# Perceiver layer on one core: weights asked for five chunks ahead, three partition passes dealt anew, and the last stores issued by ScalarE

## What is computed

```
x = x + xattn(layernorm(x), ctx)        # top-k channel gate, conv, sigmoid
x = x + attention(layernorm(x))         # wq, wk, wv, rope, softmax, wo
h = layernorm(x)                        # x: 16 x 64 tokens x 2048, fp32
logits = h @ gate_w.T                   # 8 experts, best 2, softmax of the two
out = x + h @ base_w.T + base_b + 2 * sum_e w_e * (h @ lora_A[e].T) @ lora_B[e].T
```

## Time and profile before

| | us |
|---|---|
| median of 3 runs | 2206.58 (2205.01 to 2207.42) |
| the profiled execution's own time | 2208.99 |
| its span | 2207.2 |
| PE busy in the span | 1883.5 (85%) |
| DVE busy | 1437.4 (65%) |
| ACT busy | 1129.0 (51%) |
| POOL busy | 1113.9 (50%) |
| mean granted clock of PE | 0.957 |

### The profile page before, as it was taken

One profiled execution on the slowest core, in us unless ns is written; L12 is line 12 of the kernel. 1 busy time (PEld: TensorE's weight loads), 2 busy tenths in 40 slices (PEclk: granted clock), 3 DMA queues, 4 the chain that ended last, 5 costly groups with the idle time before them and its releaser, 6 DMA issues. The chain is left out here.

```text
span 2207.2 us, 37947 instructions
## 1 busy us (share of the span) xinstructions
PE 1883.5 (85%) x14129; PEld 1512.1 (69%) x14129; DVE 1437.4 (65%) x2226; ACT 1129.0 (51%) x2523; POOL 1113.9 (50%) x935
## 2 busy tenths in 40 slices
PE   4678789777734568999999999999999899998979
PEld 4666667666521167888878888888778787776867
DVE  5898999999999898544436401344457448655443
ACT  7999999999946674332323322223324233322212
POOL 2333344444337406666655555566645455785434
PEclk9899999999976779999999999999999999999989
DMA  9999999999801036422254442222353352675565
GB/s 388 393 384 400 356 356 352 337 346 356 318 30 77 19 98 197 130 86 87 78 183 143 143 132 96 86 86 84 128 165 126 115 205 92 209 243 164 169 213 194
DMA packets 169912, 428.56 MB, mean 194 GB/s; under 512 B 16896, under 2 KB 45824, under 8 KB 168064
## 3 DMA queue, kind: packets, MB, share of 16 engines
q1 hardware_dynamic: 164832, 416.10, 54.6%
q10 hardware_dynamic: 4608, 8.39, 1.0%
q0 software_dynamic: 288, 1.64, 0.2%
HBM read 392.51 MB, written 33.55 MB: 193 GB/s over the span
## 5 line engine op out<-in xcount | busy, mean ns | idle before, releaser
L1566 POOL TENSOR_TENSOR t<-t,t 128x512 fp32r<-128x512 f32 (+1 forms) x472 | 658.0, 1408 | 640.4 <-ACT t L1555 568.1
L2371 PE MATMUL ps<-t,t 128*128 128x512 f32 x1792 | 718.8, 401 | 36.3 <-POOL t L1566 30.9
L2372 PE MATMUL ps<-t,t 128*128 128x512 f32 x1792 | 703.9, 393 | 0.0
L2373 PE MATMUL ps<-t,t 128*128 128x512 f32 x1792 | 703.5, 393 | 0.0
L1555 ACT ACTIVATE t<-t 128x512 fp32r<-128x512 f32 (+1 forms) x472 | 281.4, 608 | 680.7 <-PE ps L2373 297.9
L883 PE MATMUL ps<-t,t 128*128 128x128 bf16 (+1 forms) x5889 | 406.4, 223 | 165.5 <-DVE t L566 154.3
L883 PEld LDWEIGHTS ps<-t,t 128*128 128x128 bf16 x5889 | 348.7, 101 | 243.8 <-DVE t L566 214.2
L566 DVE TENSOR_SCALAR t<-t,t 128x1601 bf16<-128x1601 f32 x453 | 465.6, 1054 | 6.0 <-PE ps L883 1.4
L2371 PEld LDWEIGHTS ps<-t,t 128*128 128x128 f32 x1792 | 339.8, 190 | 125.8 <-POOL t L1566 47.5
L795 ACT ACTIVATE t<-t,t 128x1601 int8<-128x1601 f32 x256 | 419.0, 1637 | 8.0 <-DVE t L725 7.9
L2373 PEld LDWEIGHTS ps<-t,t 128*128 128x128 f32 x1792 | 339.8, 190 | 73.1
(11 more groups left out here) (276 smaller groups left out, 1971.2 us busy)
## 6 DMA issues: line engine op xcount, KB each, us to landing
t<-ctxT SPq DMA_DIRECT2D x256, 800.5 KB, 6.7
t<-wqkv SPq DMA_DIRECT2D x192, 256.0 KB, 3.2
t<-wb SPq DMA_DIRECT2D x144, 256.0 KB, 3.6
t<-wo SPq DMA_DIRECT2D x128, 256.0 KB, 4.6
t<-xT SPq DMA_DIRECT2D x48, 256.0 KB, 7.0
t<-x1d SPq DMA_DIRECT2D x32, 256.0 KB, 4.9
x2d<-t SPq DMA_DIRECT2D x32, 256.0 KB, 2.0
t<-x2d SPq DMA_DIRECT2D x8, 1024.0 KB, 7.4
```

What stands on the lines that cost most here:

```text
L1566: e.tensor_tensor(wlo[r][:, 0:nk, :], raw[RAW_OF[n, 0]][:, 0:nk, :], wh[r][:, 0:nk, :].bitcast(F32), ALU.subtract).then_inc(w_lo, 1)
L2371: e.matmul(bank[:, :], wh[r][:, q, :], xl, start=(begins and q == 0), stop=False)
L2372: e.matmul(bank[:, :], wlo[r][:, q, :], xh, start=False, stop=False)
L2373: m = e.matmul(bank[:, :], wh[r][:, q, :], xh, start=False, stop=(ends and q == nk - 1))
```

## The change

1. **Five ahead.** From the first FFN chunk on SP asks at chunk n for chunk n + 5 (at the first for n + 3 to n + 5) in place of n + 3. The store of o[15] is moved ahead of that first asking. The buffers stay six, their waits too.
2. **Stores.** The 24 stores of q5 and q4 (three of the result's four quarters) go from SP to ACT (lines 2189, 2190 and 2192 of the changed kernel), after ACT's high part of the chunk three ahead. The p2 stores stay on SP.
3. **LN1_PLAN** runs the sums, centring and scaling up to four chunks earlier; the first half's gate steps stand one chunk later.
4. **LN2.** Sums of squares of columns 256 to 511 go from DVE (q2, q3) to POOL: 15 adds of 128x256, each behind the one before (ssq1 to ssq15, places 6 to 13). The steps from t1 to n3b stand one place earlier.
5. **Passes.** a2's low part goes from POOL (8 of 128x512, places 64 to 71) to DVE (2 of 128x2048, places 66 and 69); n3's low parts start at place 32, not 29; q3's eight stand three places apart (54 to 75); s1l1 at 84, not 82.
6. **Gate of the second half.** l2 and l3 at 72 and 73 (73 and 74 before), ka at 77 (78), w at 86 (83), w1 at 87 (84), r at 89 (85), r1 at 90 (86).

```diff
-LN1_PLAN = "x0 - x1 - x2 - x3 - s0 - s1 - s2 - s3 - t0 c0 - c1 c2 - c3 c4 q0 - q1 - q2 - q3 - t1 v - r g0 g1 g2 g3 - g4"
+LN1_PLAN = "x0 - x1 - x2 - x3 s0 - s1 - s2 s3 - t0 c0 c1 - c2 c3 c4 q0 - q1 - q2 - q3 t1 v - r g0 g1 g2 g3 - g4 - - - - -"
...
+for _t in range(1, 16):
+    PARTS_AT.setdefault(6 + _t // 2, []).append(f"ssq{_t}")
...
+AHEAD = 5
...
         if s == "t1":
-            e.wait_ge(l_sum, 8 * i + (8 if i < 2 else 4))
+            e.wait_ge(l_sum, 8 * i + (8 if i < 2 else 2))
+            if i == 2:
+                e.wait_ge(p_part, P_NO["ssq15"] + 1)
...
+        if s[:3] == "a2l":
+            e.wait_ge(a_part, A_NO[f"a2h{g}"] + 1)
+            e.wait_ge(v_part, V_NO["s1a1"] + 1)
+            e.tensor_tensor(ATL[:, far, :], AF1[:, far, :], XH_[:, near, :].bitcast(F32), ALU.subtract).then_inc(v_part, 1)
...
-        if s[:3] == "a2l":
-            e.wait_ge(a_part, A_NO[f"a2h{t // 4}"] + 1)
-            e.wait_ge(v_part, V_NO[f"s1a{t // 4}"] + 1)
-            e.tensor_tensor(ATL[:, 8 + t, :], AF1[:, 8 + t, :], XH_[:, t, :].bitcast(F32), ALU.subtract).then_inc(p_part, 1)
+        if s[:3] == "ssq":
+            sq = AF0[:, :, 256:512]
+            e.wait_ge(l_sq, 8 + t // 4 + 1)
+            if t > 1:
+                e.wait_ge(p_part, P_NO[s])
+            e.tensor_tensor(R1[:, 256:512], sq[:, 0] if t == 1 else R1[:, 256:512], sq[:, t], ALU.add).then_inc(p_part, 1)
...
+    def asked(n):
+
+        if n < N_FFN:
+            return [n + 3]
+        return range(n + 3 if n == N_FFN else n + AHEAD, n + AHEAD + 1)
...
+                if (p, c) == (P_FFN, 0):
+                    store(p - 1)
                 if CH0[p] + c:
-                    weights_sync(e, CH0[p] + c + 3)
+                    for n in asked(CH0[p] + c):
+                        weights_sync(e, n)
...
-                if c == 0 and p and PROJ[p - 1][0] in ("o", "p2", "q5", "q4"):
+                if c == 0 and p and p != P_FFN and PROJ[p - 1][0] in ("o", "p2"):
                     store(p - 1)
...
+    def result_scalar(e, p):
+        kind, _, i, _ = PROJ[p]
+        e.wait_ge(bank_out, BANK_NO[p] + 1)
+        if kind == "q5":
+            e.dma_start(out[:, 1, 8 + i, :], last_rc[i][:, :]).then_inc(d_end[0], 16)
+            e.dma_start(out[:, 0, 8 + i, :], U[i][:, :]).then_inc(d_end[0], 16)
+        if kind == "q4":
+            e.dma_start(out[:, 1, i, :], V[i][:, :]).then_inc(d_end[0], 16)
...
                 weights_scalar(e, CH0[p] + c + 3)
+                if p and c == 0 and PROJ[p - 1][0] in ("q5", "q4"):
+                    result_scalar(e, p - 1)
```

More of the change, by code:

```diff
@@ L143 @@
 LN_PLAN = " x0 - x1 - x2 - x3 - s0 - s1 - s2 - s3 - - t0 c0 - c1 - c2 - c3 c4 q0 - q1 - q2 - q3 - n0 t1 n1 v n2 r n3 - n4"
-LN1_PLAN = "x0 - x1 - x2 - x3 - s0 - s1 - s2 - s3 - t0 c0 - c1 c2 - c3 c4 q0 - q1 - q2 - q3 - t1 v - r g0 g1 g2 g3 - g4"
+LN1_PLAN = "x0 - x1 - x2 - x3 s0 - s1 - s2 s3 - t0 c0 c1 - c2 c3 c4 q0 - q1 - q2 - q3 t1 v - r g0 g1 g2 g3 - g4 - - - - -"
 EXPERTS_PLAN = "l0 l1 l2 l3 - l4 - u - ka kb kc x - w - w1 - r - r1"
 LN2_AT = {0: ["x0", "t0"], 1: ["x1"], 3: ["x2", "c0"], 4: ["x3"], 5: ["c1"], 7: ["c2"], 8: ["c3"], 9: ["c4"], 10: ["q0"], 11: ["q1"],
-          13: ["q2"], 15: ["q3"], 16: ["t1"], 17: ["v"], 18: ["r"], 19: ["g0"], 20: ["g1"], 21: ["g2"], 23: ["g3"]}
@@ L150 @@
-PARTS_AT = {24: ["n3a0"], 25: ["n3b0"], 26: ["n3a1", "n3h0"], 27: ["n3b1"], 28: ["n2a0", "n3h1"], 30: ["n2a1", "n2h0"],
-            31: ["s1a0"], 32: ["n2h1"], 34: ["s1a1"],
+          15: ["t1"], 16: ["v"], 17: ["r"], 18: ["g0"], 19: ["g1"], 20: ["g2"], 22: ["g3"]}
+PARTS_AT = {23: ["n3a0"], 24: ["n3b0"], 25: ["n3a1", "n3h0"], 26: ["n3b1"], 28: ["n2a0", "n3h1"], 29: ["n2a1", "n2h0"],
+            31: ["s1a0", "n2h1"], 34: ["s1a1"],
             45: ["q3a0"], 46: ["q3b0"], 47: ["q3h0"], 48: ["q3a1"], 49: ["q3b1"], 50: ["q3h1"], 52: ["n2l0"], 54: ["n2l1"],
-            62: ["a2h0"], 63: ["a2h1"], 78: ["s1h0"], 79: ["s1h1"], 80: ["s1l0"], 82: ["s1l1"]}
+            62: ["a2h0"], 63: ["a2h1"], 66: ["a2l0"], 69: ["a2l1"], 78: ["s1h0"], 79: ["s1h1"], 80: ["s1l0"], 84: ["s1l1"]}
@@ L154 @@
+for _t in range(1, 16):
+    PARTS_AT.setdefault(6 + _t // 2, []).append(f"ssq{_t}")
 for _t in range(8):
[L155 to L159, removed]
+    PARTS_AT.setdefault(32 + _t, []).append(f"n3l{_t}")
+    PARTS_AT.setdefault(54 + 3 * _t, []).append(f"q3l{_t}")
@@ L163 @@
+EXPERTS_AT = {47: ["l0"], 48: ["l1"], 72: ["l2"], 73: ["l3"], 75: ["l4"], 76: ["u"], 77: ["ka"], 79: ["kb"], 81: ["kc"], 82: ["x"],
+              86: ["w"], 87: ["w1"], 89: ["r"], 90: ["r1"]}
 PARTS = [s for k in sorted(PARTS_AT) for s in PARTS_AT[k]]
-BY_POOL = ("n3l", "q3l", "a2l")
+BY_POOL = ("n3l", "q3l", "ssq")
 V_NO = {s: k for k, s in enumerate(s for s in PARTS if s[2] != "h" and s[:3] not in BY_POOL)}
@@ L1943, in parts_gpsimd @@
     def parts_gpsimd(e, s):
-        t = int(s[3])
+        t = int(s[3:]) if s[2] != "h" else 0
         if s[:3] == "n3l":
@@ L1972, in part_there @@
         if kind == "lb" and h == 1 or kind == "q4" and i == 0 and c < 2:
-            e.wait_ge(p_part, P_NO[f"a2l{4 * c + 3}"] + 1)
+            e.wait_ge(v_part, V_NO[f"a2l{c}"] + 1)
     def experts_tensor(e, i, s):
@@ L1987, in experts_tensor @@
             if s == "l2" and i:
-                e.wait_ge(p_part, P_NO["a2l7"] + 1)
+                e.wait_ge(v_part, V_NO["a2l1"] + 1)
             bank = PS_ if i == 0 and c < 2 else b1
@@ L2108, in store @@
                 e.dma_start((x2d if kind == "o" else out)[:, h, i, :], (ev if kind == "o" else rc)[s][:, :]).then_inc(d_out[s], 16)
[L2109 to L2113, removed]
         def residual(p):
@@ L2164, in mm_sync @@
                     e.dma_start(part(AF0, k // 4, k % 4, 4), part(xT[:, 1, :, :], k // 4, k % 4, 4)).then_inc(d_xq[k // 4][0], 16)
-                if c == 0 and p and PROJ[p - 1][0] in ("o", "p2", "q5", "q4"):
+                if c == 0 and p and p != P_FFN and PROJ[p - 1][0] in ("o", "p2"):
                     store(p - 1)
-        store(len(PROJ) - 1)
         for s in range(2):
@@ L2201, in mm_scalar @@
                 e.activation(U[i][:, :], PA[p % 3][:, :], ACT.Copy).then_inc(p1_out, 1)
+        result_scalar(e, len(PROJ) - 1)
     def conv_gpsimd(e):
```

## The result

The changed kernel took 2173.67 us, the median of four runs (2172.76 to 2175.91), beside 2205.86 for the kernel before (2205.01 to 2207.42). The ratio is 0.9855, interval 0.9838 to 0.9872: faster by 32.2 us, where 42.3 were forecast. It lies inside the range, on the poor side of the middle.

A forecast was written before the change was run, and what follows sets the result against it. PE stood or ran slow for 61.8 us, through waits, mostly on late weights, and the lower clock. Terms 4.4 + 7.0 + 7.2 + 9.2 + 14.5 = 42.3 us took the median from 2206.58 to 2164 us, range 2153 to 2185.

The forecast's parts named there:

- x and q5: Stretch to 2153.8: without SP's store wait, loads wait for buffers alone; rounds of 9.13 us become 6.7, 14.5 us won.
- q3: Stretch to 2085.2: w's later place removes PE's 5.9 us wait and slow clock, loads come earlier; 9.2 us won.
- p7 and q6: Stretches to 2019.3: logits no longer wait for POOL passes, kept stores still set the pace; 7.2 us won (3 to 9.5).
- signs of an error: Adds over 1 us, t1 wait over 3, ACT idle before q5 stores, loads of 5 us, over 45 of 61.8 unused.
- The layer norm: End of the first layer norm: earlier steps remove PE's 5.9 us wait on DVE's last split; 4.4 us won (2 to 7).
- scaling and chunks move together, so this stays: First layer norm: lateness of the weights' chain through ACT, 2.9 us plus some 1.0 before, remains: 3.9 us lost.
- p1 and p2: Stretch 1788.5 to 1906.5: POOL's adds take 0.75 us, loads no longer stand behind stores; 7.0 us won (3 to 10).
- the sum's lateness: In p2, the sum, 6 us after PE finished p2[1], delays loads; called the worst of 13.1 us lost.
- Rival 1: Transfers bound x and q5: rounds of 7.9 us, 5 won there in place of 14.5, total 2174 us; chance 0.15.
- Rival 2: DVE and POOL slow each other: p1 and p2 win nothing, p7 and q6 only 3, total 2175 us; chance 0.15.
- Rival 3: Buffers, not the store's wait, hold q5's loads, so only the passes count: 28 won, total 2179 us; chance 0.05.
- Rival 4: ACT's stores block the high parts, eating all 42.3 us won: 2215 us and over; chance 0.03.

The follow-up runs named there:

- c: The kernel before, with five ahead and the q5 and q4 stores on ACT, all passes old: 2191.5 us, ratio 0.9919 to the kernel before.
- d: The changed kernel's passes alone, with loads three ahead and all stores on SP: 2192.1 us, ratio 0.9917 to the kernel before.
- f: The changed kernel with the first norm's scaling passes g0 to g4 two places apart: 2168.9 us, ratio 0.9816 to the kernel before.
- e: The changed kernel with the squares q2 and q3 on DVE again, no adds on POOL: 2171.7 us, ratio 0.9827 to the kernel before.
- a: The changed kernel with loads three ahead and o[15]'s store back behind that asking, stores still on ACT: 2174.0 us, ratio 0.9833 to the kernel before.
- b: The changed kernel with the q5 and q4 stores back on SP, still five ahead: 2174.4 us, ratio 0.9835 to the kernel before.
- k: The changed kernel with a2's low part on POOL again (places 64 to 71), logits at 72 and 73: 2183.3 us, ratio 0.9893 to the kernel before.
- g: The changed kernel with w, w1, r and r1 back at places 83 to 86: 2176.0 us, ratio 0.9848 to the kernel before.
- i: The changed kernel asking five ahead up to q3 and three ahead from x[0] on: 2172.6 us, ratio 0.9838 to the kernel before.
- h: The changed kernel without q5's second store (8 stores of 256 KB left out): 2178.8 us, ratio 0.986 to the kernel before.

## Why the prediction was right, and where it was off

**The sign, the range, and where the time comes from: right.** The forecast was that the time comes from SP's store wait in x and q5 and from passes that PE waited for; 32.2 of 42.3 us came, about half from each part (c and d). Two of the terms, p2 and q3, came by another way than the text gave, and q3's size is luck in so far. All that the text said would show it came: no wait on DVE before the logits or w, no wait of SP at a q5 store, rounds of (2118.6 - 2062.7) / 8 = 7.0 us at a clock of 1.00, POOL without a gap over the adds, and 106.9 - 103.0 = 3.9 us of PE idle in p7 and q6 with landings as SP's long wait. None of its signs of an error did: the adds took under 1 us but for one, PE stood 1.4 us at t1, 30.0 us stayed unused where 45 was the bound. ACT's stores in x and q5 went out within 1 us of a rounding, and loads took 4.1 us. Two slips of the working change nothing: the poor ends of the five terms add up to 20 us and not 21, and eight chunks at places 32 to 39 hold two small ones, so that POOL has some 19.0 us there where PE has 17.7, with the same excess of 1.3. The misses, stage by stage:

**The layer norm: 4.4 forecast, 1.9 won.** The failed step is "scaling and chunks move together, so this stays", with 3.9 us left. The passes g0 to g3 stand in four neighbouring places before and after, and the sums of the next weights come late between them on DVE. From 1697 to 1712 the clock was 0.89. Timeline of after, DVE and POOL, which answers to the earlier trace rows:

```profile
1699.43 2.28 DVE L1858 TENSOR_TENSOR t<-t,t 128x2048 fp32r<-128x2048 f32 x1
...
1702.35 1.57 DVE L2263 TENSOR_TENSOR t<-t,t 128x512 f32<-128x512 f32 x1
1703.85 2.28 DVE L1858 TENSOR_TENSOR t<-t,t 128x2048 fp32r<-128x2048 f32 x1
...
1707.59 5.50 POOL L1569 TENSOR_TENSOR t<-t,t 128x512 fp32r<-128x512 f32 x4 [4.22 <-ACT t L1558]
```

The last split ends at 1706.1, 13.8 us earlier than before, but the weights' low parts still come late: four in one row from 1707.6, after POOL had stood 4.2 us for ACT. 6.8 were left and not 3.9. The waits are 4.2, near the forecast. The clock took at most 15 x (1 - 0.89) = 1.7 of the other 2.6; the rest is not explained (f, at a clock of 1.00, leaves 57.8 - 250 x 0.227 = 1.0 unused with waits of 0.8). I had priced the lateness of the chain and not the slow clock with it. f shows the cause: with gaps between the passes the stretch is 5.7 us shorter. The 13.6 us of room were there; the plan used them for the passes' end and not for their spacing.

**p1 and p2: 7.0 forecast, 2.6 won.** By cuts p1 lost 2.4 and p2 won 4.7. In p1 the mechanism was as forecast, a POOL that is just the bound, and the add of 0.75 was near: fourteen of the fifteen took 725 to 742 ns. The first took 2.80:

```profile
1808.08 2.80 POOL L1966 TENSOR_TENSOR t<-t 128x256 f32<-128x256 f32 x1
1810.83 1.29 POOL L1569 TENSOR_TENSOR t<-t,t 128x512 fp32r<-128x512 f32 x1
1812.10 1.60 POOL L1966 TENSOR_TENSOR t<-t,t 128x256 f32<-128x256 f32 x2
```

Two adds and a low part then took 2.83 us (from 1810.83 to 1813.66), as forecast 2.8, against PE's 2.7; 2 us in all was forecast and 2.4 lost. The place that t1 won does not show as a gain: e, with DVE's reductions, has p1 at 56.2. In p2 the failed step is that the worst of the loss is "the sum's lateness" that is "handed on to loads": the loads still stand behind the store of two projections back (31.5 us, above), and the depth is not what p2 gained by: with five ahead and the old passes (c) it takes 62.5 us, with three ahead and the new ones (a, d) 56.8. What p2 won is the new passes'; which of them was not tried. What it still loses is at DVE's passes, which ACT waits for before the high part of a weight:

```profile
1864.79 1.92 ACT L1937 ACTIVATE t<-t 128x2048 fp32r<-128x2048 f32 x1 [3.90 <-DVE t L1906]
1866.62 0.61 ACT L1558 ACTIVATE t<-t 128x512 fp32r<-128x512 f32 x1
...
1876.14 1.74 POOL L1957 TENSOR_TENSOR t<-t,t 128x512 fp32r<-128x512 f32 x1
1876.66 3.38 DVE L1913 TENSOR_TENSOR t<-t 128x2048 f32<-128x2048 f32 x1
1877.85 3.31 POOL L1569 TENSOR_TENSOR t<-t,t 128x512 fp32r<-128x512 f32 x1
```

The text had this wait in the 6.1 us it left; 10.5 minus p1's 2.9 is 7.6 in p2. No run moved these passes, so how the 7.6 split between ACT's wait and POOL's low parts stays open.

**p7 and q6: 7.2 forecast, 5.4 won.** Kept landings are the long wait in after (68.1 us, 26 times; before, over the whole stage, 66.8 and 26 times), the distance does nothing there (a 109.7, b 109.6), and k shows that a2's low part on POOL ahead of the moved logits costs 5 to 9 us. The term is off by 1.8, less than this stage moves by itself between kernels with the same passes there. After's 106.9 lies near the low end of their 106.5 to 110.2, where 5.4 won is near the top of some 2 to 6: that it came so near the forecast is partly luck.

**q3: 9.2 forecast, 9.6 won, the size right and the reason not.** The text gave nearly the whole to w's later place. g puts that at 2.1 us. With w back at 83 the wait is 1.9 and not 5.9, so DVE's search before w must itself have come earlier. The timelines show it: the operation that w waits for, before and after (q3 begins at 2019.3 and at 2006.6), with s1l1's pass (lines 1921 and 1930):

```profile
2034.88 2.29 DVE L1921 TENSOR_TENSOR t<-t,t 128x2048 fp32r<-128x2048 f32 x1
2037.99 0.75 DVE L2070 TENSOR_TENSOR t<-t 128x32 f32<-128x32 f32 x1
...
2020.65 0.19 DVE L2081 TENSOR_TENSOR t<-t 128x32 f32<-128x32 f32 x1
2023.14 3.38 DVE L1930 TENSOR_TENSOR t<-t,t 128x2048 fp32r<-128x2048 f32 x1
```

It ended 19.5 us after the start of q3 before, and 14.2 after. s1l1's 2.29 us stood ahead of it and now stand behind (84, before 82); ka stands one place earlier (77, before 78), and the loads are five ahead. c and d say that passes did most of it (63.7 and 57.1), and that the loads are worth about the 1.2 us forecast (d and a 57.1 and 57.2, after 56.1). The places were not tried apart, and no run moves w alone: it may be that w's later place would have won as much by itself, the two being remedies for one wait.

**x and q5: 14.5 forecast, 12.7 won.** The store wait was the cause (d: 70.6 us with it, b and a: 54.9 and 52.5 without). The forecast round was 6.7 and came as 7.0. The step that is missing is the residual's load, which stands in the queue that the stores had left: the prediction went through the loop of one weight buffer and did not ask what stands behind the five loads that now wait for buffers. i takes the wait away and the round is 52.0 / 8 = 6.5, a little better than the 6.7 forecast.

**The rule of the Trainium skill** (DMA: Bandwidth & Descriptors, "Issuing engines are not separate DMA queues") had been read to mean at most 1 us a round for the stores' move alone: by it d and a, which differ in that alone there, would lie at most 8 us apart in x and q5. They lie 70.6 - 52.5 = 18.1 apart, 2.3 a round, since the move also took a wait away in front of loads. Beside five ahead (b against after) the move is worth nothing, which the rule would allow.

**Rival 1, the transfers bound x and q5:** not this. The share rose from 0.63 to 0.77 and loads took 4.1 us in place of 3.8 (medians in this stretch); but a and i have a share of 0.83 and 0.81 in less time, and h, with eight stores fewer, is at 0.64 in more. It had the round at 7.9. **Rival 2, DVE and POOL slow each other:** in part, and smaller: one add of 2.80 in place of 0.73 beside DVE's centring (line 1841, three passes in 10.0 us), and a low part of 3.31 in place of 1.29 beside a pass of DVE of 3.38. The rule named there, of the Trainium skill (SBUF — State Buffer, "Who interferes with whom"), is that the one that issues second is blocked for the first's whole instruction. This trace agrees to 0.2 us, by the rows shown under p2: DVE's pass at 1876.66 would start when POOL's at 1876.14 ends (1877.88) and take its 2.28, to 1880.2 (it ended at 1880.0), and POOL's at 1877.85 would start then and take its 1.29, to 1881.3 (1881.2). **Rival 3, five ahead is three in practice:** no. With the stores on SP five ahead is worth 2192.1 - 2174.4 = 17.7 us (d against b). It is worth nothing only where the stores are off SP (a). **Rival 4, slower by ACT's stores:** not seen. ACT's waits in x and q5 are almost all for sums of two loads; none stands at a store:

```profile
ACT t L1558 <- DVE t L1546: 42.5, 14, 5.8
ACT t L1558 <- PE ps L2398: 2.3, 2, 2.0
```

## What to carry to other kernels

When a wait in a queue holds loads back, asking for them earlier and moving the waiting instruction to another queue are two remedies for one loss: test each alone before adding both up. After either, list what else stands in that queue behind loads that wait for buffers; a small load that another engine needs early, like a residual, can become the new wait. Where passes of an in-order engine are put into gaps of a pipeline, try them one place apart first: room at the end did not help here, where the next weight stood behind four passes in a row.

## What the runs showed of the chip that was not expected

- Fewer transfers, more time: with q5's second stores, eight in all, left out, x and q5 took 59.8 us in place of 55.9 and the wait for the residual rose from 9.2 to 21.6 us. That it is the loop above is argued from the timelines and from i, which breaks the loop and has 52.0; why h falls deeper into it than after was not tried.
- An add on POOL of 128x256 took 0.73 us, and 2.80 where it began beside DVE's centring. DVE's two reductions, from 1813.15 to 1820.83, did not slow the adds: two took 1.61 to 1.62 us beside them and 1.59 to 1.62 after, with DVE idle. Between the 0.47 of 128x128 and the 1.29 of 128x512 the time goes by columns.
- Where a pass of DVE with two inputs and one of POOL met, both records grew, and each by what was left of the other's: 2.28 to 3.38 us on DVE, 1.29 to 3.31 on POOL.
- With three waits of PE, 4.2 us in all and 3.0 the longest, the granted clock was 0.89 from 1697 to 1712, which is 3.3 us at the 1.2 GHz level and costs up to 1.7 us more; with two waits of 0.8 us in all it stayed at 1.00.
